# The value product in three 16-bit products, the weights' split in five pieces, and a new order of the step

## What is computed

```python
q = conv_silu(x @ Wq); k = conv_silu(x @ Wk); v = conv_silu(x @ Wv)   # 4 taps, 16 heads of 128, 128, 256
q, k = l2norm(q), l2norm(k)
alpha, beta = sigmoid(x @ Wa), sigmoid(x @ Wb)
def step(state, inp):                      # for each token
    state = state * at
    err = vt - einsum('bhkv,bhk->bhv', state, kt)
    state = state + bt * einsum('bhk,bhv->bhkv', kt, err)
    return state, einsum('bhkv,bhk->bhv', state, qt)
x = x + outs @ Wo
# third part: routed = sum over experts of comb[token, expert] * (sigmoid(x @ wg) * (x @ wu)) @ wd
```

## Time and profile before

| | |
|---|---|
| median of 3 runs | 884.89 us (880.30 to 886.42) |
| the profiled execution | 882.86 us, of which the span of the profile is 881.1 us |
| mean granted clock of TensorE | 0.979 of full speed |
| 32 steps of the recurrence | about 20 to 650 us of the span, 18.6 to 18.7 us a step in the stretches shown below |
| busy | TensorE 811.9, VectorE 707.2, ScalarE 630.2, POOL 501.6 us |

### The profile page before, as it was taken

The page is one execution under the profiler, slowest core; times in us unless marked ns, Lnnn a source line. Parts: engine busy times, 40 slices in busy tenths (PEclk is TensorE's granted clock), DMA queues, the critical chain, the costliest instruction groups (busy, mean ns, idle before and its releaser), DMA issues.

```text
span 881.1 us, 21906 instructions
## 1 busy us (share of the span) xinstructions
PE 811.9 (92%) x7458; PEld 526.2 (60%) x7458; DVE 707.2 (80%) x1221; ACT 630.2 (72%) x1052; POOL 501.6 (57%) x633
## 2 busy tenths in 40 slices
PE   3789999999999999999999999999889999989997
PEld 1356766767766777666677667776665333333353
DVE  7588888888888888888888888888566888874747
ACT  3588888888888888888888888888342377765522
POOL 7556959668585775868668596655612223331300
PEclk9799999999999999999999999999999999977999
DMA  5313011010110101001010110000000060000000
GB/s 140 99 27 85 2 38 38 2 37 0 36 35 0 36 0 36 11 25 36 0 36 0 36 36 0 12 2 2 1 2 24 9 108 24 21 21 18 8 24 25
DMA packets 35650, 23.97 MB, mean 27 GB/s; under 512 B 6260, under 2 KB 34644, under 8 KB 35469
## 3 DMA queue, kind: packets, MB, share of 16 engines
q1 hardware_dynamic: 32845, 18.98, 7.7%
q0 software_dynamic: 2752, 4.29, 2.4%
HBM read 22.64 MB, written 1.08 MB: 27 GB/s over the span
## 4 chain that ended last, share of the span: by engine, by line
PE 68%; DVE 14%; issue 9%; ACT 4%; POOL 3%; DMA 1%; SPq 1%; DVEq 1%; ACTq 0%; POOLq 0%
PE psum L1316 13%; PE psum L1345 12%; PE psum L1515 6%; DVE y L1030 6%; PE psum L1673 4%; PE psum L1401 3%; PE psum L1391 3%; DVE ux L1010 3%; PE psum L1423 2%; PE psum L1623 2%; PE psum L1659 2%; PE psum L1430 2%; PE psum L1638 2%; PE psum L1433 2%; PE psum L1763 1%
## 5 line engine op out<-in xcount | busy, mean ns | idle before, releaser
L1030 DVE SCALAR_TENSOR_TENSOR y<-psum,cwh,y 128x508 f32<-128x508 f32 (+2 forms) x384 | 281.6, 740 | 21.6 <-ACT y L728 15.5
L487 POOL TENSOR_TENSOR sql<-sq,sqh 128x1024 f16<-128x1024 f32 x32 | 68.4, 2138 | 135.7 <-ACT sq L775 135.7
L1345 PE MATMUL psum<-wo,vt 128*128 128x256 f32 x512 | 126.0, 389 | 1.2 <-DVE y L1030 1.0
L728 ACT ACTIVATE y<-psum,cwh 128x512 f32<-128x512 f32 x128 | 99.3, 776 | 29.5 <-PE psum L1316 28.7
L501 POOL TENSOR_TENSOR ct<-lm,levels 128x256 f16<-128x256 f32 x160 | 111.0, 711 | 6.8 <-DVE lm L1053 6.8
L1345 PEld LDWEIGHTS psum<-wo,vt 128*128 128x128 f32 x512 | 92.3, 190 | 11.9 <-DVE y L1030 2.0
L1168 DVE TENSOR_REDUCE mx<-psum 128x4 f32<-128x1024 f32 x64 | 77.6, 1220 | 12.7 <-PE psum L1638 12.4
L849 ACT ACTIVATE et<-psum 128x1024 f32<-128x1024 f32 x64 | 65.4, 1023 | 28.9 <-PE psum L1659 27.9
L1010 DVE TENSOR_TENSOR ux<-ux,psum 128x512 f16<-128x512 f16 x64 | 44.0, 687 | 51.9 <-PE psum L1433 50.8
L1316 PE MATMUL psum<-xth,whi 128*128 128x512 f16 x256 | 78.5, 389 | 6.6 <-POOL wlo L468 2.3
L1316 PE MATMUL psum<-xtl,whi 128*128 128x512 f16 x256 | 78.3, 388 | 0.0
(11 more groups left out here) (220 smaller groups left out, 1957.7 us busy)
## 6 DMA issues: line engine op xcount, KB each, us to landing
wraw<-in_L_attn_Wv SPq DMA_DIRECT2D x32, 128.0 KB, 2.7
wo<-in_L_attn_Wo SPq DMA_DIRECT2D x16, 256.0 KB, 2.8
wraw<-in_L_attn_Wk SPq DMA_DIRECT2D x16, 128.0 KB, 2.5
wraw<-in_L_attn_Wq SPq DMA_DIRECT2D x16, 128.0 KB, 2.9
moved<-avs SPq DMA_DIRECT2D x128, 16.0 KB, 1.8
x<-in_x SPq DMA_DIRECT2D x8, 128.0 KB, 4.0
maskrow<-in_mask_row POOLq DMA_DIRECT2D x1, 1024.0 KB, 5.4
xt<-in_ctx SPq DMA_DIRECT2D x1, 1024.0 KB, 6.4
```

What stands on the lines that cost most here:

```text
L487: g.tensor_tensor(lo, f, hi, ALU.subtract).then_inc(sq_split, 1)
L728: s.activation(y[:, n], ubank[n % 2].rearrange("p (j t) -> p j t", j=NB), ACT.Identity, scale=cwh[:, (a.c // 2) % 2, n, TAPS - 1:TAPS], bi ...
L1030: v.scalar_tensor_tensor(out=y[:, n, :, sh:], in0=u[:, :, 0:T - sh], scalar=cwh[:, (a.c // 2) % 2, n, TAPS - 1 - sh:TAPS - sh], in1=y[:, n ...
L1345: mm = t.matmul(ubank[n][:, j * H:(j + 1) * H], vt[:, r, vc, (2 * n + j) * T:(2 * n + j + 1) * T], wo[:, hr, vc, :], start=(vc == 0), stop ...
```

## The change

1. `z(n)`: values and output weights are split into a high and a low 16-bit part (`vth`, `vtl`, `woh`, `wol`), and each fp32 matmul becomes three 16-bit ones: high x high, high x low, low x high. For it ScalarE runs the values' Silu twice, once into fp32 `vt` and once into 16-bit `vth` (`v_high`), POOL subtracts (`v_low_`), and `zcopy` divides by 64, since the output weights are scaled like the others.
2. The weights' split becomes five pieces in two slots: scale the projection weights and the output weights (slot of `k.at(4)`), then round both, subtract both (slot of `f = k.at(3)`). `wo` has one buffer; SyncE's wait for the value products is gone. `lm_hi` and the rounding of the weights are a `tensor_copy` instead of an addition of zero.
3. The order of the slot changes on every engine.
4. `spread` and `combt` have 128 rows instead of 16; the others are zero.

```diff
-    spread = np.zeros((2 * NE, WT * P), np.float32)
+    spread = np.zeros((P, WT * P), np.float32)
@@ SyncE's queue
                     if nxt.valid():
-                        need(sp, w_split, nxt.head)
+                        need(sp, w_split, nxt.head * 2)
                         load_w(nxt.head)
-                        if nxt.c // 2 >= 2:
-                            sp.wait_ge(z_psum, nxt.at(-4).count(2, 4))
-                        load_wo(nxt.head, (nxt.c // 2) % 2)
+                        load_wo(nxt.head)
@@ POOL
+            def split_scale(h):
+                pool.wait_ge(w_loaded, h * 64 + 64)
+                g.tensor_tensor(w, w, c64[:].to_broadcast([P, TILES * CH * P]), ALU.mult).then_inc(w_high, 1)
+            def split_scale_out(h):
+                pool.wait_ge(wo_loaded, h * 16 + 16)
+                g.tensor_tensor(o, o, c64[:].to_broadcast([P, 2 * H]), ALU.mult).then_inc(w_high, 1)
+            def split_high(h, ring, user):
+                    pool.wait_ge(z_psum, user.count(2, 4))
+                g.tensor_copy(wh, w).then_inc(w_high, 1)
+                g.tensor_copy(oh, o).then_inc(w_high, 1)
+            def split_low(h, ring):
+                g.tensor_tensor(wl, w, wh, ALU.subtract).then_inc(w_split, 1)
+            def split_low_out(h, ring):
+                g.tensor_tensor(ol, o, oh, ALU.subtract).then_inc(w_split, 1)
+                def v_low_(b0):
+                    pool.wait_ge(v_act, b0.count(2, 2))
+                    g.tensor_tensor(lo, f, hi, ALU.subtract).then_inc(v_split, 1)
-                    g.tensor_tensor(lmh[...], lm[...], zero[...], ALU.add).then_inc(lm_high, 1)
+                    g.tensor_copy(lmh[...], lm[...]).then_inc(lm_high, 1)
                 cut(b, 1)
+                next_high(f)
+                next_scale(k.at(4))
+                part_high(b0)
+                part_rest(b0)
+                part_middle(b0)
+                part_low(b0)
                 cut(b, 2)
-                parts_()
-                lm_hi()
+                next_low_out(f)
                 cut(b, 3)
-                lm_lo()
+                next_scale_out(k.at(4))
+                v_low_(b0)
                 cut(b, 4)
-                split_next()
-                sq_low_()
+                next_low(f)
+                lm_hi(b)
+                lm_lo(b)
+                sq_low_(a)
                 cut(b0, 0)
@@ ScalarE, order of the slot
-                v_silu()
-                ccopy(4)
+                v_silu(b0)
+                v_high(b0)
+                ccopy(c, 4)
 ...
-                exp(0)
-                exp(1)
-                bias(2)
-                bcopy(2)
+                exp(b0, 0)
+                bcopy(b, 2)
+                exp(b0, 1)
+                bias(a, 2)
                 y0copy(c)
-                k_silu()
-                ycopy()
-                bias(3)
-                bcopy(3)
-                square_high()
-                square()
+                k_silu(a)
+                bias(a, 3)
+                ycopy(c)
+                bcopy(b, 3)
+                square(a)
+                square_high(a)
@@ VectorE, order of the slot
-                lmul_later(1)
-                add_out_later(1)
+                add_out(d, 1)
+                lmul(b, 1)
+                lmul(b, 0)
                 level_c(c, 4)
 ...
-                level_c(6)
                 tap(a, 1, 1)
+                level_c(c, 6)
 ...
-                tap(2, 1)
-                tap(2, 2)
-                residual()
-                level_b(2)
-                tap(2, 3)
-                lmul(0)
-                tap(3, 1)
-                tap(3, 2)
-                add_out(0)
-                tap(3, 3)
-                level_b(3)
+                tap(a, 2, 1)
+                residual(c)
+                tap(a, 2, 2)
+                level_b(b, 2)
+                tap(a, 2, 3)
+                tap(a, 3, 1)
+                tap(a, 3, 2)
+                tap(a, 3, 3)
+                level_b(b, 3)
+                add_out(c, 0)
@@ TensorE
-                            mm = t.matmul(ubank[n][:, j * H:(j + 1) * H], vt[:, r, vc, ...], wo[:, hr, vc, :], start=(vc == 0), stop=(vc == 1))
+                            t.matmul(o, vth[:, r, vc, ts], woh[:, hr, vc, :], start=(vc == 0), stop=False)
+                            t.matmul(o, vth[:, r, vc, ts], wol[:, hr, vc, :], start=False, stop=False)
+                            mm = t.matmul(o, vtl[:, r, vc, ts], woh[:, hr, vc, :], start=False, stop=(vc == 1))
@@ TensorE, order of the slot
-                grams_later(1)
-                outp(0)
-                outp(1)
-                b_ux_later(3)
+                grams(b, 1)
+                b_t1(c, 3)
+                outp(d, 0)
+                b_ux(c, 3)
+                outp(d, 1)
                 z(b, 0)
 ...
                 proj_(a, 2)
                 y0(c)
-                residual()
-                grams(0)
-                b_ux(2)
+                b_ux(b, 2)
+                residual(c)
                 proj_(a, 3)
                 y1(c)
-                b_t1(3)
+                grams(b0, 0)
```

More of the change, by code:

```diff
@@ L782, in square_high, with v_silu, v_high @@
                     s.activation(sqh[:], kq[:, a.c % 2], ACT.Square, scale=4.0).then_inc(sq_high, 1)
-                def v_silu():
+                def v_silu(b0):
+                    if not b0.valid():
+                        return
+                    act.wait_ge(tapped[2], b0.count(3, 3))
+                    act.wait_ge(tapped[3], b0.count(3, 3))
+                    need(act, v_split, b0.count(1, 0))
+                    s.activation(vt[:], y[:, 2:4].rearrange("p a j t -> p a (j t)"), ACT.Silu).then_inc(v_act, 1)
+                def v_high(b0):
                     if not b0.valid():
@@ L1112, in slot @@
+                keys = k.i is None and k.c in (STEPS - 1, STEPS)
+                b4 = (k.c - STEPS + 1) * 4
+                add_out(d, 1)
+                lmul(b, 1)
+                lmul(b, 0)
+                level_c(c, 4)
                 if k.i is None and k.c == STEPS:
                     moments(dve, 1, slice(0, NB))
-                floor()
-                terms()
-                level_b0(1)
-                level_b0(0)
-                level_c(5)
-                tap(0, 1)
-                tap(0, 2)
@@ L1121, in slot @@
[L1121 to L1134 removed]
+                floor(b0)
+                terms(b0)
+                level_b0(b, 1)
+                level_b0(b, 0)
@@ L1392, in grams, with b_first @@
                     mm.then_inc(kq_psum, 1)
[L1394 to L1404 removed]
+                def b_first(b):
                     if not b.valid():
@@ L1568, in slot @@
[L1568 to L1588 removed]
+                    hh = 1 - m
@@ new lines, in k_proj @@
+                    need(pe, k_stack, 2 * (bb - 1))
+                    if m == 1:
+                        need(pe, v_ready, 2 * (bb - 1))
+                    for g2 in range(2):
+                        o = kbank[bb % 2][hh][:, g2 * H:(g2 + 1) * H]
+                        t.matmul(o, wks[:, 2 * hh + g2], ctxs[:, bb], start=True, stop=False)
+                        mm = t.matmul(o, biasr[:, 1, 2 * hh + g2], maskr[:, bb], start=False, stop=True)
+                    mm.then_inc(k_psum, 1)
+                keys = k.i is None and k.c in (STEPS - 1, STEPS)
@@ new lines, in slot @@
+                b4 = (k.c - STEPS + 1) * 4
+                grams(b, 1)
[3 more added lines that the diff above has]
+                outp(d, 1)
+                z(b, 0)
+                c_t1(c, 4)
+                z(b, 1)
+                c_ux(c, 4)
+                norms(b0)
+                b_first(b)
+                c_t1(c, 5)
+                proj_(a, 0)
+                if keys:
+                    k_proj(b4 + 0, 0)
+                    k_proj(b4 + 0, 1)
@@ new lines, in slot @@
+                c_ux(c, 5)
+                b_t1(b, 1)
+                proj_(a, 1)
+                gate_products()
+                b_ux(b, 1)
+                turn(b0)
+                c_t1(c, 6)
+                exponents(b0, 0)
+                c_ux(c, 6)
+                exponents(b0, 1)
+                if keys:
+                    k_proj(b4 + 1, 0)
+                    k_proj(b4 + 1, 1)
+                    v_proj(b4 + 0)
+                b_t1(b, 2)
+                proj_(a, 2)
+                y0(c)
```

406 lines of the change are left out of this document (198 added, 208 removed).

## The result

Before 885.33 us (880.3 to 886.42), changed 904.48 us (901.12 to 909.47), medians of 4 runs each; ratio 1.023, 95% interval 1.017 to 1.030. The forecast was 867.5 us, 2% faster; the kernel became 2.3% slower. The profiled executions have spans of 881.1 and 904.2 us, so the traces hold 23.1 us to find.

What follows compares the result with a forecast made beforehand. A ring of TensorE and VectorE was taken to bound the kernel. 29 steps x -0.55 = -16.0, spread -3.4, start +2.0: -17.4 on the profiled 882.9 gives 865.5, as median 867.5 us, 2.0% faster; whole range 854 to 885.

Steps and rivals of the forecast that it cites:

- The ring: Chain of waits between TensorE and VectorE, taken as the bound; forecast to close 0.55 to 0.6 us earlier a step.
- the value product: TensorE's z(n): 24 16-bit matmuls at 0.112 us, 2.7 us a step instead of 3.62, so 0.93 us given up.
- my walk: Event-by-event timing of one slot after the change, setting Ln, terms and first tap earlier; steps of some 18.05 us.
- The rest is eaten by ScalarE: The second Silu, ahead of the Ln, was to leave 0.55 to 0.6 us a step of TensorE's 0.93.
- The other moves: Reordered VectorE, TensorE and SyncE work in the slot, claimed to be the same work on the ring, priced at nothing.
- Parts ... hidden, with nothing to spare: POOL's parts behind next_high in odd slots: done at 394.4, wanted by TensorE's transpose at 394.5, so no cost.
- steps that differ between odd and even by over 0.5 us: One of the signs listed in advance that would show the forecast wrong.
- the start: First split with output weights in front, 0.8 to 2.0 us, and second Silu in unfilled slots: +2.0 us taken.
- Nothing that the ring needs stands behind them: Output-weight loads on SyncE's queue wait only for the split, one slot earlier, with half a step to spare.
- The spread: Last stage: 128 rows remove TensorE's gaps around the 16-row matmul, 18 x 0.19 = 3.4 us; lower bound nothing.
- (A): Rival: POOL is the bound, copies at 1.9 us; -0.2 to -0.3 us a step, 876.2 us in all; chance 0.2.
- (B): Rival: slower, ScalarE's chain not started earlier, first tap 0.3 us later a step, 892.2 us; chance 0.12.

Runs made afterwards that it cites:

- no_second_silu: end_unroll without ScalarE's second Silu from the third step on (values wrong from there): 859.24 us, ratio 0.972 to before.
- order_only: end_unroll with the fp32 value product, its one Silu and fp32 output weights put back; new order and 128-row spread kept: 885.03 us, ratio 1.000.
- both_late: Changed kernel with the scaling and the rounding casts of the weights' split moved behind the four part operations on POOL: 882.28 us, ratio 0.998.
- end_unroll: both_unroll with both scalings of the next head's weights moved to the end of POOL's slot: 855.29 us, ratio 0.968.
- unroll_after: Changed kernel with the loop over passes of four steps written out, nothing else: 888.29 us, ratio 1.002.
- both_unroll: both_late with the loop over passes of four steps written out: 861.85 us, ratio 0.977.
- spread_before: Kernel before with the 128-row spread alone: 884.83 us, ratio 0.997.
- unroll_before: Kernel before with the loop over passes written out, nothing else: 880.79 us, ratio 0.993.
- trim_after: Changed kernel without the low part of the sums of squares on TensorE, 64 records a pass fewer: 889.59 us, ratio 1.005.

## Why the prediction was wrong

**The ring and the value product: right.** The new matmuls start 0.109 us apart (forecast 0.112), 2.6 us a step, so TensorE gives up 1.0 us, and the good steps are below the 18.05 of my walk. VectorE's wait before `level_c(4)` is 0.54 us, as forecast under 0.6:

```profile
389.70 0.69 DVE L1109 TENSOR_TENSOR ux<-ux,psum 128x512 f16<-128x512 f16 x1 [0.54 <-PE psum L1518]
```

**"The rest is eaten by ScalarE": wrong size.** I let the second Silu take 0.35 us of TensorE's 0.93. It takes 0.03 (`no_second_silu`). The wait for the `Ln` did not rise to 0.9 us but is 0.33 to 0.46 in the full steps. The walk took the `Ln` to stand behind ScalarE's table load; in the kernel before it stood idle behind it and waited for VectorE, room in which most of the second Silu fits:

```profile
391.73 0.21 ACT L754 ACTIVATE lnn<-n2m 128x8 f32<-128x8 f32 x1 [0.67 <-DVE n2m L1074]
```

**"The other moves ... priced at nothing": wrong sign, small.** They cost 0.18 us a step (`order_only`). The two errors partly cancel: 0.93 - 0.03 - 0.18 = 0.72 (0.8 with the 1.0 us measured), where the written-out kernels measure 18.50 - 17.80 = 0.70 and the forecast was 0.55. The mechanism on which the forecast rested thus holds, and between the written-out kernels it is worth 29 x 0.70 = 20 us.

**"Parts ... hidden, with nothing to spare": the wrong question.** This is the first step that failed. I asked when POOL would be through with `next_high` and whether TensorE's transpose could wait for the parts. POOL's copies were even cheaper than taken (1.04 us for a cast of 1024, forecast 1.2), so that answer was right: no full step waits for the parts. What I didn't ask is what VectorE does while POOL runs. The earlier trace rows shows POOL idle for 1.04 us until `terms` is done, and the earlier trace rows `terms` at 0.17 us: that row was measured with POOL idle beside it. The even slots I passed over altogether, though `next_scale` moved ahead of the parts there too. The prediction did name the sign, "steps that differ between odd and even by over 0.5 us", but no cause for it. Price: `both_late` against the changed kernel, 22.2 us, of which 1.6 in the start; 26.4 with the loop written out.

**"Nothing that the ring needs stands behind them": true of SyncE's queue, not of POOL's.** The loads that matter went to the DMA about as early as before (the third head's at 57.99 us against 57.62). But before, the first thing that waited for them was the split, at the end of POOL's slot; the DMA's time lay beside cuts and lows. The change puts the waiting instruction ahead of the parts. In the start POOL comes to the scaling at 57.6 us, when these loads aren't yet issued, and waits 6.28 us. I priced the start at +2.0: the first `Ln` comes 1.1 us late, and the distance from the second to the third is 8 us longer. Price: the last 6.6 us come back in `end_unroll`.

**The term that isn't in the sum: the loop's edge.** I counted instructions as time on the engine (24 products for 8) and never as length of the loop's body. The five waits of 2.2 to 2.5 us and what follows them make 3.7 to 4.3 us of step each. Price: 16.2 us (`unroll_after`) to 20.4 us (`both_late` to `both_unroll`).

**The spread: right mechanism, too many rounds.** 1.51 to 1.52 us between rounds, forecast 1.53; -3.4 us taken for 18 rounds. Fourteen rounds went from 1.72 to 1.52, but waits elsewhere take a part back: from the first spread to the last it is 63.24 us before, 60.81 in the changed kernel and 60.96 in `spread_before`, 2.3 to 2.4 us less; the medians of `spread_before` say 2.7 (0.1 to 5).

The sum in this form: 885.0 for before; 29 x -0.70 = -20.3 for the steps; -4.2 for the loop form of before; -2.3 for the spread gives 858.2, and `end_unroll` measures 855.3. From there back to the changed kernel the measured steps are 6.6 for the scaling ahead of the cuts, 20.4 for the loop and 22.2 for the place of the split, 904.5 in all; these are differences of medians, taken in this order, and so add up by themselves. From the first `Ln` to the last, where the rest of the kernel can't blur them, the traces have 568.0 us for `unroll_before`, 548.6 for `end_unroll`, 554.7 for `both_unroll`, 576.6 for `both_late` and 595.8 for the changed kernel: 6.1, 21.9 and 19.2 us for the three.

A part of the 23.1 us between the two traces is none of this. From the last `Ln` to the first spread the changed kernel takes 198.8 us against 195.1, and over all traces of the study this stretch takes 190.3 to 201.2 us, in kernels of either kind. In it the granted clock of TensorE is lower for some microseconds. Here are two stretches with the same work (us, busy of PE, PEld, DVE, ACT, POOL, clock), of before and then of the changed kernel, 1.9 us apart. I can't show that the change has a part in it, and it bounds what one trace's span can tell.

```profile
790.00:799.00 9.00, 8.05 (x74) 4.68 (x72) 2.65 (x8) 4.80 (x7) 2.18 (x3) 0.80 0.03 7
```

```profile
812.50:823.40 10.90, 9.95 (x74) 5.91 (x72) 3.01 (x9) 4.79 (x7) 2.19 (x3) 0.66 0.06 15
```

Of the rivals none was it: POOL did not become the bound (A), nor did ScalarE's chain (B). Slower came by three mechanisms of which the prediction names none. Without them the change brings more than was forecast: 855.29 against 880.79 us for the two written-out kernels, 2.9% and not 2.0%.

## What to carry to other kernels

When an operation moves to another place on its queue, ask three things of the new place: what it waits for and who stands behind it, what runs on VectorE beside it (here a 0.17-us operation with two SBUF inputs lasted to the end of POOL's reading operation, up to 1.76 us), and what the duration in the old trace was measured beside. When a change multiplies instructions in a loop, compare the packets of the instruction queue and the first work behind the branch. A good change can measure as a loss for reasons that small repairs take away, here three moved lines and a loop written out: look at the best step before dropping it.

## What the runs showed of the hardware

- A loop body of TensorE with some 1433 records of products and loads a pass runs round with 0.2 us at the edge; 64 records more cost 2.1 to 3.7 us there and what the other engines lose behind it, and the page's instruction packets go from 32 to 78. 64 records fewer in the changed kernel undo both (`trim_after`). For this kernel the limit lies between; other instructions of the body (waits, register work) are not in these records. The Trainium skill (Runtime: NRT & Kernel Launch, Instruction fetch mechanics) says that a taken branch whose target is no longer held forces a fetch before the engine goes on. The packets agree with it. That the gap is such a fetch is read from them and from the two lengths, since no row shows the fetch itself; the price is that of these rows.
- Written out, the same steps show no such gap, with 61 to 64 packets for the whole kernel: straight code came in time.
- VectorE's operation with two SBUF inputs, begun while a reading operation of POOL ran, ended within 0.03 us of its end, whether that was an addition, a scaling or a one-input cast of 1024 elements; a memset held nothing.
- POOL's cast of 128x1024 takes 1.04 us, the same copy written as an addition of zero 1.89 us.
